# Tokenizer and scan stage of a four-stage kernel in one block, on one SBUF map drawn by hand

## The chip, the cores and the metric

The kernel runs on one core of one Trainium2 chip. The metric is the device time of one launch in microseconds (us), the median of three runs. The engines are TensorE (PE in the profile, its weight loads PEld), VectorE (DVE), ScalarE (ACT), GpSimd (POOL) and SyncE (SP), which here only issues DMAs and waits. Each engine runs its own instruction list in order; they meet at semaphores.

## The reference, cut to what matters

```python
# x [32,3,112,112], txt [32,32,192]
h = tokenizer(x)              # convs, wavelet packet, three depthwise+pointwise layers, layernorm; cls row first
h = concatenate([h, txt], 1)  # [32, 82, 192]: 1 cls + 49 patches + 32 text rows for each image
h = h + scan_layer(layernorm(h))   # selective scan (16 states, 384 channels), then a gated FFN
h = h + moe_layer(layernorm(h))    # 12-head attention, top-2 of 8 experts
# scan_layer(x): hn = rmsnorm(x) ; z = (hn @ W_in.T) * sigmoid(hn @ W_gate.T)
#   dt_in, Bm, Cm = split(z @ W_xproj.T) ; dt = softplus(dt_in @ W_dt.T + b_dt)
#   state[l] = exp(dt*A) * state[l-1] + (dt*z)*Bm ;  y = sum_s state*Cm + D*z ; ...
```

## The kernel before, in words

All values are float32. `H` [82 rows, 32 images, 192] stays in SBUF from the first stage to the last. There are four stages: `tokenizer`, `mamba` (the scan stage), `attention` with the routing, and `experts`. `mamba` and `attention` begin with a small block of their own, `row_stats`, for the mean and variance of each row of H. Each block ends at a barrier of all engines, and the SBUF and PSUM of one stage are given back before the next takes its own.

**Tokenizer.** Four chunks (`CH = 4`) of eight images (`IM = 8`) go through a software pipeline of seven waves (`w = 0..6`). In a wave DVE does the nine depthwise taps of several layers, one channel tile at a time (`dw`, L165 to L175: one TENSOR_SCALAR and eight SCALAR_TENSOR_TENSOR, accumulated in the PSUM bank psF). For the other tile ACT makes nine products (`weigh`, L337) in a ring of 14 and POOL adds them up (`add_up`, L478, eight dependent additions). PE does the pointwise layers (L232), and for the last layer 32 matmuls a chunk (L292), whose result comes out with the patches as rows. DVE takes these rows to `T0` (`take_rows`: L406 copies with a bias, L410 and L413 statistics), POOL makes the roots (`roots`, L465 and L467, POW), and DVE normalizes (`norm_rows`: eight L419, one L422, one L424). SP moves each finished chunk to H (L199).

In wave 5 DVE does: take_rows(1), the taps of the second fusion layer for chunk 3, the taps of the third for chunk 2, norm_rows(0). In wave 6: take_rows(2), the third layer's taps for chunk 3, norm_rows(1); then take_rows(3), norm_rows(2), norm_rows(3). When the chunks have landed, SP clears the semaphores and all engines meet (`retire`, L45).

**Scan stage.** `row_stats` (L529) takes 32 BN_STATS (L549) and 32 BN_AGGR (L552) on DVE and roots on POOL, while SP issues ten loads of weights and constants (L607). After a barrier DVE prepares constants, POOL makes the remaining roots (L1031 to L1040), and the 8 rounds of four images (`G = 4`, N = 328 columns) begin. A helper `program` writes the order: 16 steps (`STATE`), and in step s of round i each engine calls `step` (the scan of state s), `post` for the round before and `pre` for the round after. Round 0's `pre` has no scan beside it. Its parts by step number: 0 ACT makes `hn` (L861); 2 PE transposes it, ACT makes `hT`; 3, 4, 5 for each third of the channels two projections on PE (RG and RI, L756), a Tanh on ACT, a product `z` on DVE (L964); 6 two more products X1 and X0 (L764), `Bs` and `P3` on ACT, `R` on DVE (L969); 7 the low parts of P3; 8 and 9 step sizes on PE (L743), Relu, Abs and Exp on ACT; 10 Ln and two copies on ACT, then three additions on POOL (L1048, L1050, L1052) for `dt`; 11 one product on POOL for `dtz` (L1055). Then POOL makes `Bx` (L1075), ACT the decays (L935), and DVE runs the first scan (L1006). The projections of one pair of PSUM banks wait for the `z` before them.

`Bs` goes to memory and back as a broadcast `Bb` (L696, L700), and SP also zeroes an eighth of the expert buckets in each round (L705).

**Attention stage, its end.** For each of 8 rounds DVE's `place` writes the bucket slots of the tokens (L1553), and POOL scatters the rows with eight indirect DMAs (L1604). `slot` is one tile, so in the last round `place` waits for the scatters of the round before. POOL also adds the residual to H each round (L1620); SP writes H out (L1210).

Of the kernel before, what the change touches and what calls it, by code (L numbers as in the profile page):

```python
# [15 lines left out]
B = 32  # L16
# [28 lines left out]
def retire(nc, sems):  # L45

    for s in sems:
        nc.sync.sem_clear(s)
    nc.all_engine_barrier()
# [26 lines left out]
def tokenizer(nc, H, xcol, w_pl, w_pg, had, pw_mix, w96, vecs, pwb_row, lng_row, lnb_row, cls_row, txt):  # L76


    CH = 4
    IM = B // CH  # L80
    NP = IM * PATCHES
    ROW = GRID + 1
    IMG = ROW * ROW
    PADC = IM * IMG
    EDGE = ROW + 1
    ROWS = IM * ROW - 1
    with ExitStack() as ctx:
        def sb(name, shape, dt=F32):
            return ctx.enter_context(nc.sbuf_tensor(name, shape, dt))
# [12 lines left out]
        vec = sb("vec", [128, V_N])  # L102
# [6 lines left out]
        PRODUCTS = 14  # L109
# [14 lines left out]
        psC = ctx.enter_context(nc.psum_tensor("psC", [128, 3, BANK], F32))  # L124
        psA = ctx.enter_context(nc.psum_tensor("psA", [128, 2, BANK], F32))
        psB = ctx.enter_context(nc.psum_tensor("psB", [128, 2, BANK], F32))
        psF = ctx.enter_context(nc.psum_tensor("psF", [128, BANK], F32))
# [13 lines left out]
        s_mv = sem("a_mv"); s_rs = sem("a_rs"); s_t1 = sem("a_t1"); s_padp = sem("a_padp"); s_nh = sem("a_nh"); s_out = sem("a_out"); s_cls = sem("a_cls")  # L141
# [40 lines left out]
        ctx.callback(retire, nc, sems)  # L182
        block = ctx.enter_context(nc.Block())

        @block.sync
        def _(sp):
# [9 lines left out]
            sp.dma_start(H[1 + PATCHES:S, :, :], txt.rearrange("b t c -> t b c")).then_inc(s_cls, 16)  # L196
            for c in range(CH):
                sp.wait_ge(s_t1, c + 1)
                sp.dma_start(H[1:1 + PATCHES, c * IM:(c + 1) * IM, :], T0[:, c * IM:(c + 1) * IM, :]).then_inc(s_out, 16)  # L199
            sp.wait_ge(s_out, 16 * CH)  # L200
            sp.wait_ge(s_cls, 32)

        @block.tensor
        def _(pe):
# [32 lines left out]
            for w in range(WAVES):  # L237
                if w + 1 < CH:
                    conv(w + 1)
                if w < CH:  # L240
                    if w == 0:
                        pe.wait_ge(s_small, 16 * 3)
# [30 lines left out]
                if 0 <= w - 2 < CH:  # L273
# [6 lines left out]
                    pair(psA, wf[:, 2], lambda k: dense(DF[1], k)).then_inc(s_f[1], 1)  # L280
                if 0 <= w - 3 < CH:
# [14 lines left out]
        @block.scalar  # L296
        def _(act):
# [6 lines left out]
            act.wait_ge(s_small, 48)  # L304
# [35 lines left out]
            for w in range(WAVES):  # L340
                if w + 1 < CH:
                    gelu(w + 1)
                if 0 <= w - 1 < CH:
# [47 lines left out]
        @block.vector  # L391
        def _(v):
# [6 lines left out]
            v.wait_ge(s_small, 48)  # L399
            v.wait_ge(s_rows, 48)  # L400

            def take_rows(c):

                for n in range(c * IM // 2, (c + 1) * IM // 2):
                    v.wait_ge(s_f[2], n + 1)
                    v.tensor_tensor(T0[:, 2 * n:2 * n + 2, :], f3_bank[n % 3].rearrange("p (j c) -> p j c", j=2),  # L406
                                    rows[:, 0:1, :].broadcast_to([PATCHES, 2, D]), ALU.add).then_inc(s_t0, 1)
                v.wait_ge(s_t0, (c + 1) * IM // 2)
# [18 lines left out]
            for w in range(WAVES):  # L427
# [5 lines left out]
                if 0 <= w - 1 < CH:  # L433
# [3 lines left out]
                    dw(v, own, PF[0], DF[0], (0,), w - 1, V_F_DW, s_dwf[0])  # L437
                if 0 <= w - 4:
                    take_rows(w - 4)
                if 0 <= w - 2 < CH:  # L440
# [3 lines left out]
                    dw(v, own, PF[1], DF[1], (0,), w - 2, V_F_DW + 18, s_dwf[1])  # L444
                if 0 <= w - 3 < CH:
# [64 lines left out]
G = 4  # L510
# [1444 lines left out]
```

## Time and profile before

| | us |
|---|---|
| median of 3 runs (lowest, highest) | 1613.34 (1612.24, 1614.69) |
| the profiled execution: its time | 1608.27 |
| its span (first to last instruction) | 1606.4 |
| last tap of the tokenizer ends | 241.07 |
| tokenizer's last DVE instruction ends | 264.8 |
| first statistics of the scan stage begin | 272.4 |
| first scan of round 0 begins | 334.46 |
| last scatter of the attention stage is issued | 1305.8 |
| first instruction of the experts' stage on DVE | 1311.5 |

| engine | busy us | share of the span |
|---|---|---|
| PE | 1265.3 | 79% |
| DVE | 1033.7 | 64% |
| POOL | 764.3 | 48% |
| ACT | 708.1 | 44% |

Times of single instructions below are from this one profiled execution, whose time is 5.1 us under the median of the runs. Busy shares are averages over four stages with different limits; the places that matter here are the seam at 240 to 335 us and the end of attention at 1270 to 1312 us.

### The profile page before, as it was taken

How to read it: one execution, taken by the hardware profiler on the slowest of the kernel's cores; microseconds unless marked ns; L12 is line 12 of the kernel's file. 1: busy time of each engine (PE TensorE's matmuls, PEld its weight loads, DVE VectorE, ACT ScalarE, POOL GpSimd, SP SyncE). 2: the span in 40 equal slices, each digit the busy share in tenths (PEclk: the TensorE clock that was granted, in tenths of full speed). 3: DMA queues.
4: the chain of work that ended last, by engine and by line, in shares of the span. 5: the costliest groups of instructions: out<-in, count | busy, mean ns of one | idle time of the engine just before them, and what ended most of it. 6: DMA issues, size and time to landing. Idle time of an engine off the chain costs nothing. (4 is left out here: it accounts for less than half of the span.)

```text
span 1606.4 us, 19648 instructions
## 1 busy us (share of the span) xinstructions
PE 1265.3 (79%) x5818; PEld 834.7 (52%) x5819; DVE 1033.7 (64%) x1939; ACT 708.1 (44%) x1486; POOL 764.3 (48%) x500
## 2 busy tenths in 40 slices
PE   6786732456988989898878579888987529999996
PEld 4332321232554545455445348777876517777775
DVE  4699587168978889898898327776567512333332
ACT  1156620357758586776853135444442102222221
POOL 2038970387676676857672321144444632222222
PEclk9796775679989999999999779999797559999999
DMA  5100002123303030330300111121201112222221
GB/s 153 50 1 0 1 8 77 63 77 126 108 19 127 1 126 13 114 111 15 126 0 1 32 36 54 40 66 53 62 23 24 32 51 32 37 37 36 36 36 23
DMA packets 71571, 81.17 MB, mean 51 GB/s; under 512 B 13534, under 2 KB 63349, under 8 KB 71401
## 3 DMA queue, kind: packets, MB, share of 16 engines
q1 hardware_dynamic: 52210, 68.69, 13.7%
q0 software_dynamic: 17152, 9.24, 4.2%
q10 hardware_dynamic: 2136, 2.37, 0.5%
q8 instruction: 32, 0.52, 0.1%
q14 instruction: 41, 0.34, 0.1%
HBM read 48.93 MB, written 30.01 MB: 49 GB/s over the span
## 5 line engine op out<-in xcount | busy, mean ns | idle before, releaser
L1006 DVE TENSOR_TENSOR_SCAN hs<-b_ps,Bx 128x492 f32<-128x492 f32 x256 | 287.6, 1164 | 49.1 <-ACT b_ps L935 25.4
L1075 POOL TENSOR_TENSOR Bx<-dtz,Bb 128x984 f32<-128x984 f32 x128 | 289.3, 2279 | 56.8 <-DVE hs L1006 56.7
L935 ACT ACTIVATE b_ps<-dt,A 128x324 f32<-128x324 f32 (+1 forms) x512 | 214.1, 454 | 111.3 <-DVE hs L1006 106.0
L825 PE MATMUL b_ps<-hs,b_id 128*128 128x492 f32 x512 | 242.4, 597 | 9.2 <-DVE y L974 9.1
L1827 POOL DMA_INDIRECT out<-yt,dest x48 | 74.0, 1542 | 220.3 <-DVE yt L1814 215.0
L1015 DVE TENSOR_TENSOR hs<-hs,b_ps 128x984 f32<-128x984 f32 x128 | 150.2, 1174 | 2.6
L1708 PE MATMUL e_ps<-W,xT 97*128 (+1 forms) x384 | 138.5, 503 | 1.5 <-ACT xT L1762 1.0
L825 PEld LDWEIGHTS b_ps<-hs,b_id 128*128 128x128 f32 x512 | 94.2, 197 | 83.9 <-issue 81.6
L1800 DVE COPY hT_<-e_ps 128x768 f32<-128x768 f32 x48 | 45.9, 957 | 130.3 <-PE e_ps L1717 129.9
L1613 POOL TENSOR_TENSOR c_x<-c_x,bro 82x192 f32<-82x192 f32 x32 | 19.7, 615 | 195.2 <-DVE c_x L1456 194.7
L1727 PE MATMUL e_ps<-W,hT_ 128*128 x576 | 109.2, 327 | 0.9 <-DVE yb L1808 0.8
L795 PE MATMUL b_ps<-hfT,wug 96*128 96x328 f32 x256 | 85.2, 479 | 24.7 <-DVE av L991 24.0
L1604 POOL DMA_INDIRECT buckets<-XS,c_slot x64 | 90.4, 1412 | 27.1 <-issue 18.8
L1768 ACT ACTIVATE hb<-e_ps 128x768 f32<-128x768 f32 x48 | 38.9, 810 | 144.2 <-PE e_ps L1708 144.2
L1708 PEld LDWEIGHTS e_ps<-W,xT 97*128 97x128 f32 (+1 forms) x384 | 70.0, 192 | 55.0 <-issue 17.1
L1727 PEld LDWEIGHTS e_ps<-W,hT_ 128*128 128x128 f32 x576 | 91.4, 190 | 1.4 <-issue 1.4
L478 POOL TENSOR_TENSOR DF<-DF,prod 96x441 f32<-96x441 f32 x84 | 86.9, 1035 | 6.6
L813 PE MATMUL b_ps<-P,sel 96*128 96x328 bf16 x128 | 39.8, 312 | 59.2 <-DVE hs L1015 58.6
L795 PEld LDWEIGHTS b_ps<-hfT,wug 96*128 96x128 f32 x256 | 50.0, 203 | 64.5 <-DVE av L991 40.6
L1310 PEld LDWEIGHTS c_ps<-V,PT 82*82 82x82 f32 x768 | 69.2, 169 | 13.8 <-issue 7.6
L1762 ACT ACTIVATE xT<-e_ps,m_vec 96x128 f32<-96x128 f32 x96 | 38.4, 447 | 84.7 <-PE e_ps L1698 84.6
L1297 PE MATMUL c_ps<-kB,qT 128*82 128x328 f32 (+1 forms) x256 | 69.5, 422 | 2.0 <-DVE E L1427 2.0
(246 smaller groups left out, 2414.6 us busy)
## 6 DMA issues: line engine op xcount, KB each, us to landing
Bb<-b_rows SPq DMA_DIRECT2D x32, 656.0 KB, 7.1
buckets<-b_zero SPq DMA_DIRECT2D x8, 2288.0 KB, 15.6
xg<-buckets SPq DMA_DIRECT2D x48, 104.0 KB, 2.0
xc<-in_xcol SPq DMA_DIRECT2D x4, 1176.0 KB, 9.6
W<-in_w1d SPq DMA_DIRECT2D x8, 582.0 KB
W<-in_w2d SPq DMA_DIRECT2D x8, 576.0 KB
out<-H SPq DMA_DIRECT2D x8, 246.0 KB
H<-P SPq DMA_DIRECT2D x4, 294.0 KB
```

Of the source, the lines that this page charges most:

```text
L478: g.tensor_tensor(out, a, prod[:, (9 * n + t) % PRODUCTS], ALU.add).then_inc(s_sum, 1)
L795: mm = pe.matmul(ps[:, bank(name), 0:N], wug[:, k, w_, m * 128:(m + 1) * 128], hfT[:, k, :], start=k == 0, stop=k == 1)
L825: mm = pe.matmul(ps[:, BANK_Y + h, 0:HALF], ident[:], f2(hs[:, s % LONG])[:, h * HALF:(h + 1) * HALF], start=s == 0, stop=s == STATE - 1)
L935: a = act.activation(ps[:, BANK_A + h, c:c + w].rearrange("p (g t) -> p g t", t=S)[:, :, 1:S], dt[:, (par + t // STATE) % 2, m, g0 * S:g1 ...
L1006: v.tensor_tensor_scan(f2(hs[:, t % LONG])[:, c], ps[:, BANK_A + h, 0:HALF], f2(Bx[:, t % RING])[:, c], 0.0, ALU.mult, ALU.add).then_inc(s ...
L1015: v.tensor_tensor(hs[:, s % LONG], hs[:, s % LONG], ps[:, BANK_C + s % 2, 0:N].rearrange("p (a n) -> p a n", a=1).broadcast_to([128, NI, N ...
L1075: g.tensor_tensor(Bx[:, t % RING], dtz[:, p], Bb[:, p, t % STATE, :].rearrange("p (a n) -> p a n", a=1).broadcast_to([128, NI, N]), ALU.mu ...
L1297: mm = pe.matmul(ps[0:S, SCORES + h0 // 6, (h0 % 6) * S:(h0 % 6 + h1 - h0) * S], qT[:, par, m_, q * S:(q + 1) * S], kB[:, par, m_, q, j:j ...
L1604: g.indirect_dma_start(out=xs, out_offset=bass.IndirectOffsetOnAxis(ap=slot[:, k, c:c + 1], axis=0), in_=XS[:, par, c, :], in_offset=None) ...
L1708: mm = pe.matmul(ps[:, 1 + 2 * p + h, 0:384], xT[c_, p, k, :], W1[c_, k, bass.ds(e, 1), h * 384:(h + 1) * 384].rearrange("p a n -> p (a n) ...
L1727: mm = pe.matmul(ps[:, 7, 0:D], hT[:, p, k, :], W2[:, k, bass.ds(e, 1), :].rearrange("p a n -> p (a n)"), start=k == 0, stop=k == KF - 1)
L1827: g.indirect_dma_start(out=out, out_offset=bass.IndirectOffsetOnAxis(ap=dest[:, p:p + 1], axis=0), in_=yt[:, p, :], in_offset=None, comput ...
```

## The change

- Tokenizer and scan stage run in one block. The `retire` barrier and `row_stats` of the scan stage are gone (attention keeps its own). A function `places` gives every tile of both stages a fixed offset in one SBUF map; `vec` and `ident` are loaded once, at the start, so `ident` is one more DMA on SP's queue ahead of the image chunks. The ring of products shrinks from 14 to 13.
- The statistics are taken a chunk of eight images at a time, from H: `chunk_stats` on DVE, `chunk_roots` on POOL (one POW over both roots, 82x16, and one product).
- Hooks named `tail(point)` put round 0's first work into the tokenizer's instruction lists. DVE in wave 5: between the taps of chunk 3 and chunk 2, `chunk_stats(0)`, the halving of wzg and the cast of sel. DVE in wave 6: z of the first third inside take_rows(2), z of the second third ahead of the last taps; the third z and the memset ahead of norm_rows(3). POOL after wave 5: `chunk_roots(0)`. ACT ahead of its last nine products: `hn`. PE ahead of the last 32 matmuls: `pre` of steps 2, 3, 4. After the tokenizer DVE does R, the limit on A, `chunk_stats` 1 to 3, and then round 0's additions and product for dt and dtz, which were POOL's.
- `norm_rows(w - 5)` moves from the end of DVE's wave to its beginning.
- Loads: wzg, wx, wdt and oh are issued once the tokenizer's middle tiles are free (s_h at 4); A, wo and wdn after chunk 1 has gone to H; wug after chunk 3 has. SP clears the tokenizer's semaphores in round 0 once four engines have left it (`s_left`), ahead of the first zeroing of buckets.
- Attention: `slot` gets two halves, and the wait of the last `place` is gone; the last round's residual addition moves from POOL to DVE, after DVE's program.

```diff
-    for s in sems:
-        nc.sync.sem_clear(s)
-    nc.all_engine_barrier()
...
-        PRODUCTS = 14
+PRODUCTS = 13
...
+            sp.dma_start(ident[:], eye).then_inc(s_small, 16)
...
+                if 0 <= w - 5:
+                    norm_rows(w - 5)
                 if 0 <= w - 4:
                     take_rows(w - 4)
+                if w == WAVES - 1:
+                    tail("last taps")
...
+                if w == WAVES - 2:
+                    tail("last but one taps")
                 if 0 <= w - 3 < CH:
...
-                if 0 <= w - 5:
-                    norm_rows(w - 5)
             take_rows(CH - 1)
             norm_rows(CH - 2)
+            tail("last rows")
             norm_rows(CH - 1)
...
+            def chunk_stats(c):
+                a = slice(c * IM, (c + 1) * IM)
+                v.wait_ge(tok.s_out[c], 16)
+                for b in range(c * IM, (c + 1) * IM):
+                    n = own.did(v.bn_stats(st[:, b % IM, :], H[:, b, :]))
+                own.need(n)
+                for b in range(c * IM, (c + 1) * IM):
+                    n = own.did(v.bn_aggr(mv[:, b, :], st[:, b % IM, :]))
+                own.need(n)
+                own.did(v.tensor_scalar(r12[:, a], mv[:, a, 1], 1.0 + 1e-6, 1e-5 * 1e-6, ALU.mult, ALU.add))
+                own.did(v.tensor_scalar(r1[:, a], mv[:, a, 1], 1e-5, None, ALU.add))
+                own.did(v.tensor_scalar(negm[:, a], mv[:, a, 0], -1.0, None, ALU.mult))
+                own.need(own.n)
+                v.sem_inc(s_var, 1)
...
+            tok.vector(v, tail)
+            v.sem_inc(s_H, 2)
+            pre(0, 0, 6, None)
+            v.wait_ge(s_wA, 16)
+            v.tensor_scalar(f2(A[:]), f2(A[:]), 80.0, None, ALU.min).then_inc(s_A2, 1)
+            for c in range(1, CH):
+                chunk_stats(c)
+            program(v, first, step, pre, post, lambda last: drain(last, 1), done=(3, 4, 5, 6))
...
+            def chunk_roots(c):
+                a = slice(c * IM, (c + 1) * IM)
+                g.wait_ge(s_var, c + 1)
+                g.tensor_tensor(root[:, :, a], root[:, :, a], nh[:], ALU.pow).then_inc(s_root, 1)
+                g.wait_ge(s_root, c + 1)
+                g.tensor_tensor(nb[:, :, a], root[:, :, a], negm[:, a].rearrange("p (a b) -> p a b", a=1).broadcast_to([S, 2, IM]),
+                                ALU.mult).then_inc(s_r1, 1)
...
-                if isinstance(p, int) and p == ROUNDS - 1:
-                    v.wait_ge(s_sc, p * (16 * 2 * G))
-                v.tensor_copy(slot[:], sf[:]).then_inc(s_slot, 1)
+                v.tensor_copy(slot[:, p % 2], sf[:]).then_inc(s_slot, 1)
```

## Rows read from the trace of the kernel before

**Rows 1.** Windows: busy us (instructions) of PE, PEld, DVE, ACT, POOL; TensorE's granted clock; DMA

```profile
260.00:300.00 40.00, 5.71 (x16) 3.58 (x16) 18.09 (x76) 5.13 (x10) 13.18 (x11) 0.50 0.29 82
300.00:334.00 34.00, 13.42 (x37) 7.00 (x36) 1.98 (x4) 15.64 (x27) 12.06 (x8) 0.70 0.45 149
...
390.00:446.00 56.00, 48.75 (x168) 27.31 (x168) 48.87 (x52) 39.99 (x94) 38.66 (x20) 0.97 0.28 91
```

**Rows 2.** Timeline of the seam, 241 to 335 us: start, duration, what, [idle before <- releaser]

```profile
263.07 1.75 DVE L424 TENSOR_TENSOR P<-P,rows 49x1536 f32<-49x1536 f32 x1
...
272.43 8.41 DVE L549 BATCH_NORM_STATS2 b_st_stats<-H 82x6 f32<-82x192 f32 x32
...
280.87 2.21 DVE L552 BATCH_NORM_AGGREGATE b_mv<-b_st_stats 82x2 f32<-82x6 f32 x32
...
289.05 0.31 POOL L1031 TENSOR_SCALAR b_negm<-b_mv 82x32 f32<-82x32 f32 x1 [2.78 <-DVE wzg L956]
...
312.21 0.49 DVE L969 TENSOR_TENSOR R<-b_ps,P 64x328 f32<-64x328 f32 x1 [2.84 <-ACT P L876]
...
321.60 1.01 ACT L895 ACTIVATE ax<-ax 128x984 f32<-128x984 f32 x1
...
329.68 2.28 POOL L1055 TENSOR_TENSOR dtz<-dt,z 128x984 f32<-128x984 f32 x1
...
334.46 2.25 DVE L1006 TENSOR_TENSOR_SCAN hs<-b_ps,Bx 128x492 f32<-128x492 f32 x2 [21.77 <-POOL Bx L1075]
```

**Rows 3.** Timeline of POOL, waves 4 to 6 of the tokenizer

```profile
198.37 1.98 POOL L504 TENSOR_TENSOR PF<-L,R 96x392 f32<-96x392 f32 x2
200.31 0.96 POOL L478 TENSOR_TENSOR DF<-prod 96x441 f32<-96x441 f32 x1
201.34 7.64 POOL L478 TENSOR_TENSOR DF<-DF,prod 96x441 f32<-96x441 f32 x7
...
221.45 1.99 POOL L504 TENSOR_TENSOR PF<-L,R 96x392 f32<-96x392 f32 x2 [1.71 <-ACT R L387]
```

**Rows 4.** Timeline of DVE, waves 5 and 6 of the tokenizer

```profile
215.69 4.95 DVE L171 SCALAR_TENSOR_TENSOR psF<-PF,vec,psF 96x441 f32<-96x441 f32 x7
...
221.51 3.79 DVE L419 TENSOR_SCALAR P<-P,mv,rs 49x192 f32<-49x192 f32 x8 [0.16 <-DVE DF L171]
...
228.79 1.47 DVE L406 TENSOR_TENSOR P<-psC,rows 49x384 f32<-49x384 f32 x3
231.39 0.55 DVE L406 TENSOR_TENSOR P<-psC,rows 49x384 f32<-49x384 f32 x1 [1.12 <-PE psC L292]
231.97 2.17 DVE L410 BATCH_NORM_STATS2 st<-P 49x6 f32<-49x192 f32 x8
...
252.99 2.37 DVE L419 TENSOR_SCALAR P<-P,mv,rs 49x192 f32<-49x192 f32 x8
```

**Rows 5.** Timeline of PE: the last layer's matmuls, then round 0's projections

```profile
221.46 4.10 PE L292 MATMUL psC<-wf,DF 96*49 96x192 f32 x24 [1.19 <-DVEq L175]
...
241.18 8.42 PE L292 MATMUL psC<-wf,DF 96*49 96x192 f32 x32 [9.83 <-DVEq L175]
...
295.59 4.74 PE L756 MATMUL b_ps<-hT,wzg 96*128 96x328 f32 x8 [0.62 <-ACT hT L866]
...
306.29 2.47 PE L756 MATMUL b_ps<-hT,wzg 96*128 96x328 f32 x8 [0.66 <-DVE z L964]
```

**Rows 6.** Timeline of ACT in wave 3: the products of three tiles

```profile
137.85 15.04 ACT L337 ACTIVATE prod<-PF,vec 96x441 f32<-96x441 f32 x27
```

**Rows 7.** Timeline of POOL and DVE at the end of attention

```profile
1286.75 1.40 POOL L1604 DMA_INDIRECT buckets<-XS,c_slot  x1 [0.30 <-issue]
1292.45 1.40 POOL L1604 DMA_INDIRECT buckets<-XS,c_slot  x1 [4.29 <-DVE c_slot L1553]
...
1282.96 0.17 DVE L1548 TENSOR_REDUCE c_sf<-c_t 82x4 f32<-82x32 f32 x1
1291.97 0.17 DVE L1553 CAST c_slot<-c_sf 82x8 uint32<-82x8 f32 x1 [8.85 <-DMA buckets<-XS,c_slot]
```

More of the change, by code:

```diff
@@ L342, in _ @@
                     gelu(w + 1)
+                if w == WAVES - 1:
+                    tail("last wave")
                 if 0 <= w - 1 < CH:
@@ L659, in bank, with program @@
             return SIDE0 + PLACE[name] % SIDE
-        def program(engine, scan_first, step, pre, post, finish=lambda last: None, side_first=False):
+        def program(engine, scan_first, step, pre, post, finish=lambda last: None, side_first=False, done=(), late=lambda: None):
             def turn(i, par, s, last, has_post, has_pre):
@@ L673, in program @@
             for s in range(STATE):
-                pre(0, 0, s, None)
+                if s not in done:
+                    pre(0, 0, s, None)
             scan_first()
@@ L677, in program @@
                 turn(0, 0, s, False, False, True)
+            late()
             with engine.Fori(0, (ROUNDS - 2) // 2) as t:
@@ L690, in _, with tail @@
         def _(sp):
+            def tail(point):
+                if point == "stages over":
+                    for dst, src in ((wzg, w_zg), (wx, w_x), (wdt, w_dt), (oh, onehot)):
+                        sp.dma_start(dst[:], src).then_inc(s_w, 16)
+                if point == "last sums":
+                    sp.dma_start(A[:], a_log).then_inc(s_wA, 16)
+                    for dst, src in ((wo, w_o), (wdn, w_dn)):
+                        sp.dma_start(dst[:], src).then_inc(s_wo, 16)
+            tok.sync(sp, tail)
             for j in range(ROUNDS):
@@ L1021, in step, with tail @@
                     scan(i, s + 1)
-            program(v, first, step, pre, post, lambda last: drain(last, 1))
+            def tail(point):
+                if point == "last but one taps":
+                    v.wait_ge(tok.s_cls, 32)
+                    chunk_stats(0)
+                    v.wait_ge(s_w, 64)
+                    v.tensor_scalar(wzg[:, :, 0, :], wzg[:, :, 0, :], 0.5, None, ALU.mult).then_inc(s_cst, 1)
+                    v.tensor_copy(sel[:], oh[:, STATE:2 * STATE].rearrange("p (s a) -> p s a", a=1).broadcast_to([HD, STATE, 128])).then_inc(s_cst, 1)
+                if point == "last wave":
+                    v.wait_ge(tok.s_lr, CH)
+                    pre(0, 0, 3, None)
+                if point == "last taps":
+                    pre(0, 0, 4, None)
+                if point == "last rows":
+                    v.wait_ge(tok.s_t0, CH * IM // 2)
+                    v.memset(ps[:, BANK_A:BANK_A + 2, :], 0.0).then_inc(s_cst, 1)
+                    pre(0, 0, 5, None)
+            tok.vector(v, tail)
[6 more added lines that the diff above has]
+            program(v, first, step, pre, post, lambda last: drain(last, 1), done=(3, 4, 5, 6))
             v.wait_ge(s_H, 2 * ROUNDS + 2)
@@ L1085, in step, with tail @@
                     inputs(i, par, s + AHEAD)
+            def tail(point):
+                chunk_roots(0)
+            g.memset(nh[:], -0.5).then_inc(s_nh, 1)
+            g.wait_ge(s_nh, 1)
+            tok.gpsimd(g, tail)
+            for c in range(1, CH):
+                chunk_roots(c)
+            g.memset(zero[:], 0.0).then_inc(s_zero, 1)
             program(g, first, step, pre, post)
```

254 lines of the change are left out of this document (160 added, 94 removed).

## The prediction

> **What bounds the kernel now.** I read the stages as windows first, then the timeline of the seam, engine by engine, and then the end of attention.
>
> The windows [rows 1] show a pipeline that is nearly full in the scan rounds (DVE 48.9 and PE 48.8 of 56 us) and nearly empty at the seam: from 260 to 334 us DVE works 20.1 of 74 us, PE 19.1. The seam is a chain of single steps. The reader should see it in the timeline [rows 2]. The tokenizer's last normalization ends at 264.8. After that come the landing of its rows, the clearing of semaphores and a barrier, 7.6 us until 272.4. Statistics take until 283.1. POOL resumes at 289.05, held by constants and a second barrier: 6.0 us more. Then round 0's front runs from `hn` to `dtz` with nothing beside it, and the first scan starts at 334.46, after a wait of 21.77 us for POOL's Bx.
>
> From there on the rounds follow each other and every later stage starts from the one before it. So what the first scan gains is gained at the end, unless a round gives it back. The experts' stage is bound by PE and isn't touched.
>
> **What the change moves.** I walk DVE's new instruction list, because every other engine's new work is released by it or releases it. The start is 198.4, where POOL has the roots of chunk 0 (its next instruction starts at 198.37 [rows 3]); DVE is done with wave 4's taps by then. Clock times in this part are on the old time axis.
>
> 1. norm_rows(0), now first in wave 5. Alone its eight TENSOR_SCALARs take 2.37 us; beside two POOL additions they took 3.79 [rows 4], 1.4 more for two additions of 0.99, so about one of them got through per POOL instruction. At the new place POOL has those two additions and then sixteen more of about 1.03 us each, back to back [rows 3]. So: two of the eight at 1.0, six at 1.05, and the two long TENSOR_TENSORs at 1.75 each behind a POOL instruction of 1.0. 2.0 + 6.3 + 5.5 = 13.8 us. The lower bound is 5.9 (2.37 + 2 x 1.75: no collision); I take 13.8, since the measured row is the same instruction against the same kind of POOL instruction. POOL is held too, by at most 3.5 us, but has slack until the next rows need it.
>
> The Trainium skill has a rule for this (SBUF — State Buffer, section "Who interferes with whom"): a VectorE instruction in a two-port mode, or with two SBUF inputs beside a GpSimd instruction that reads SBUF, blocks and is blocked for whole instructions. By that rule, the row of 3.79 us agrees, norm_rows at its old place was nearly free of it and at its new place is not: it is the rule that speaks against this edit. Without it the sum would be the one with 5.9.
>
> 2. take_rows(1): 6.0 us, as from 228.79 to 234.8 (copies, a wait for a bank, statistics) [rows 4]. It now comes after norm_rows(0) instead of ahead of it, but its matmuls have long filled three banks.
> 3. Taps, chunk 3 of the second layer: 6.5 (7 x 0.71 and two ends of 0.7 [rows 4]).
> 4. chunk_stats(0): 8 x 0.263 and 8 x 0.069 from the rows of 32 [rows 2], three tiny instructions and four waits, 3.4. With the halving (0.54 before) and the cast (1.24): 5.4. H's chunk left at the end of step 1 and had 17 us to land (before it took 3.8). The weights were asked for at 168.
> 5. Taps, chunk 2 of the third layer: 6.4.
> 6. norm_rows(1), POOL idle: 6.1.
> 7. Copies of chunk 2 with the wait for the fourth bank: 3.1.
> 8. z of the first third. PE can transpose only after its last L292 of chunk 2, which the third copy freed. Transposes 0.8, hT 1.1, four products at full clock 2.5 (4.7 at half [rows 5]), z 0.5, latencies: 5.3 after the fourth copy. hn is ready by 237 (ACT waits for chunk_roots(0) behind POOL's last addition of L and R), so it isn't what is late.
> 9. Statistics of chunk 2, then z of the second third, whose products run meanwhile: 2.8 + 0.6.
> 10. Last taps: 6.5. They end near 261 instead of 241.07: this is where the inserted work goes, 20 us.
> 11. PE's 32 matmuls at half clock after its pause, 8.4, last copy 0.6: 9.0 [rows 5]. DVE waits through it; before, it did norm_rows(1) there.
> 12. Statistics 2.8, norm_rows(2) 5.9, memset and third z 1.5, norm_rows(3) 5.9: 16.1.
> 13. R and the limit on A: 0.9. PE has made X1 and X0 beside norm_rows(3).
> 14. chunk_stats 1 to 3: 3 x 3.4 = 10.2. The chain R, P3, step sizes, Exp, Ln on ACT takes 9.9 from R (312.7 to 322.6 before [rows 2]), so it is hidden under these by a hair; POOL's roots of each chunk (about 3.2: 0.156 a column from its POWs of 8 and 24 columns) trail by one and end before Bx.
> 15. Three additions and the product on DVE, 128x984 with two SBUF inputs: at the 1.14 us per 1000 columns of L424 [rows 2], 1.2 with its wait, 5.0 together. POOL took 9.3 for them (322.68 to 331.96).
> 16. First Bx 2.4.
>
> Sum: 13.8 + 6.0 + 6.5 + 5.4 + 6.4 + 6.1 + 3.1 + 5.3 + 3.4 + 6.5 + 9.0 + 16.1 + 0.9 + 10.2 + 5.0 + 2.4 = 106.1, so the first scan would start at 304.5.
>
> Two costs come earlier. The extra DMA ahead of the images: 0.5 (one issue on SP is 0.46, and PE did wait 1.8 for the images). The ring of 13: in wave 3 ACT's 27 products run without a stall [rows 6], the last at 152.3; POOL's sum that frees its place in a ring of 14 was done at 152.0, in one of 13 it is done at 153.1. 0.8 us, and ACT's later results then reach POOL's next additions with 0.2 to spare. I take both, 1.3; below it is nothing. First scan at 305.8: 28.7 us earlier.
>
> SP: b_rows goes out when its queue is past the last chunk, about 287; its broadcast lands 7 to 9 us later, before Bx at 302. wug, the clearing and the zeroing come after; the clearing of some 45 semaphores took 2.7 before. Round 1 needs its own B rows 20 us later. Hidden; if it weren't, DVE's second round would wait.
>
> **Attention.** POOL's last eight scatters start 4.29 us after the previous eight, behind the slot written at 1291.97, which waits for scatters to land [rows 7]; the values were there at 1283.1. With two halves the gap is 0.30: 4.0 us gained. The table for the experts follows the slot and moves ahead with it. The residual addition on DVE is under 2 us in a stretch where it idles 8.85.
>
> Total 32.7 us: 1575.6 for the profiled execution's 1608.27, and 1580.6 against the median, 5.1 above it.
>
> **Rivals.**
>
> A. No collision, and TensorE stays at its full clock. Step 1 costs 5.9, the 32 matmuls 5.5 (0.171 each as in the 24 of [rows 5]), the early costs are nothing: 7.9 + 2.9 + 1.3 more, 1568.5. For it: the clock was full for 24 matmuls there. Against it: the 3.79 us row, and PE pauses of 7 us ahead of both groups.
>
> B. The last waves hide nothing. The inserted pieces wait for each other (DVE for z, PE for hn, ACT for roots), and only the empty stretches vanish: 7.6 and 6.0 at the two barriers, 4.0 in attention: 1595.7. For it: steps 8 to 11 are a ring through four engines, and each of DVE's waits there delays taps that PE waits for. Against it: in my walk the products are the only wait of length, and the front between 289 and 334 is mostly steps that DVE didn't fill.
>
> C. Slower: the scan rounds start with TensorE at the lower of its two clock levels, 1.2 GHz, and it stays there. At 0.97 PE works 48.8 of 56 us [rows 1]; at 1.2 GHz that is some 95, so a round would last 40 us longer. It decides from 0.8 of a round at the low level on, which takes the 32.7 back; a whole round would give 1620. Against it: the granted clock before was 0.50 in the idle seam and still 0.89 in the first 56 us of rounds.
>
> D. The change doesn't do what it says: DVE, now with the statistics, the sums and the z's, is the only thing that matters, and new waits add up to the 32.7. No such wait is in the rows; 1612 to 1615.
>
> **How the numbers follow.** Forecast 0.60, A 0.14, B 0.20, C 0.04, D 0.02. The forecast's own range is 1574 to 1588: down by half of the collision and part of the clock, up by 2.2 for each of the two pairs of products at half clock and 3 for waits between small instructions. A reaches to 1568 and B to 1596; I leave out B's last two us and what is below 1568: 1568 to 1594. Faster by over 0.2% (3.2 us, about what a measurement of this kernel can tell from no change) 0.94, within it 0.02, slower 0.04.
>
> **What the next profile would show.** The L419 group of chunk 0 near 199 us at 8 us or more for eight (right) or near 2.4 (A). Last taps ending near 262 (if near 245, step 8 was dear for nothing; if past 268, B). The 32 last matmuls at about 8.4. DVE without a wait over 1 us between its last normalization and dt. First scan at 306. The eight-scatter groups 0.3 apart, and DVE's first instruction of the experts 32.7 earlier than 1311.45. I am wrong if the scan starts early and the rounds (56 us each) grow, or if chunk_stats waits for H to land.

## The result

| kernel | median us (lowest to highest) | ratio to the kernel before, 95% interval |
|---|---|---|
| before, beside it | 1612.79 (1610.33 to 1614.69), 4 runs | |
| changed | 1570.53 (1567.64 to 1572.95), 4 runs | 0.9743 [0.9728, 0.9758] |
| changed, on another occasion | 1571.0 (1567.61 to 1573.25), 5 runs | 0.9756 [0.9734, 0.9777] |

The change makes the kernel 40 to 42 us faster (on the second occasion the kernel before had 1610.74). Ratios leave out two executions in a slow state, one of the kernel before (1841.87 us) and one of the attention edits alone (2253.55 us), at mean granted clocks of 0.69 and 0.55 where the others have 0.87 to 0.89. The two profiled executions are 35.3 us apart (1608.27 and 1572.95). Cut at points that both have, they give:

| part (us) | before | changed | gained |
|---|---|---|---|
| start to the first scan | 334.46 | 305.37 | 29.09 |
| first scan to attention's first statistics (the rounds) | 578.94 | 576.09 | 2.85 |
| attention stage, to the experts' first DVE instruction | 398.05 | 394.79 | 3.26 |
| experts' stage | 294.95 | 294.85 | 0.10 |

The seam in windows of the changed kernel (us, busy us and count of PE, PEld, DVE, ACT, POOL, granted clock, DMA), where DVE had worked 18.1 of 40 us and 2.0 of 34 [rows 1]:

```profile
260.00:300.00 40.00, 16.95 (x58) 9.91 (x58) 32.37 (x108) 14.37 (x23) 11.13 (x7) 0.71 0.24 79
300.00:334.00 34.00, 25.81 (x80) 13.61 (x81) 30.48 (x30) 20.09 (x49) 27.60 (x15) 0.79 0.32 99
```

DVE's timeline of the changed kernel, the answers to [rows 2, 4]:

```profile
201.12 9.52 DVE L429 TENSOR_SCALAR P<-P,mv,rs 49x192 f32<-49x192 f32 x8 [4.24 <-POOL rs L481]
210.67 2.65 DVE L432 TENSOR_TENSOR P<-P,rows 49x1536 f32<-49x1536 f32 x1
213.35 1.75 DVE L434 TENSOR_TENSOR P<-P,rows 49x1536 f32<-49x1536 f32 x1
...
218.46 0.55 DVE L414 TENSOR_TENSOR P<-ps,rows 49x384 f32<-49x384 f32 x1 [1.96 <-PE ps L300]
...
228.37 2.17 DVE L1014 BATCH_NORM_STATS2 b_st<-H 82x6 f32<-82x192 f32 x8 [0.23 <-DVE DF L176]
...
239.85 2.40 DVE L429 TENSOR_SCALAR P<-P,mv,rs 49x192 f32<-49x192 f32 x8 [0.16 <-DVE DF L176]
...
252.43 0.50 DVE L1030 SCALAR_TENSOR_TENSOR z<-sg,ps 128x328 f32<-128x328 f32 x1 [3.52 <-PE ps L784]
...
261.67 0.67 DVE L176 SCALAR_TENSOR_TENSOR DF<-PF,vec,ps 96x441 f32<-96x441 f32 x1
265.29 0.55 DVE L414 TENSOR_TENSOR P<-ps,rows 49x384 f32<-49x384 f32 x1 [2.95 <-PE ps L300]
...
286.54 0.48 DVE L1035 TENSOR_TENSOR R<-ps,P 64x328 f32<-64x328 f32 x1
...
297.55 1.18 DVE L1038 TENSOR_TENSOR ax<-u,ax 128x984 f32<-128x984 f32 x1 [0.56 <-ACT ax L933]
...
301.20 1.18 DVE L1045 TENSOR_TENSOR dtz<-dt,z 128x984 f32<-128x984 f32 x1
305.37 2.25 DVE L1082 TENSOR_TENSOR_SCAN hs<-ps,Bx 128x492 f32<-128x492 f32 x2 [2.98 <-POOL Bx L1173]
```

The reader is to see three things. The eight L429 of chunk 0 take 9.52 us, those of chunk 1 at a place where POOL is idle 2.40. Between the last tap and the first scan DVE has no wait over 3 us. The wait in front of the first scan is 2.98 us for one Bx instead of 21.77. POOL beside the first rows, PE around the last matmuls (answers to [rows 3, 5]), and ACT:

```profile
204.06 7.64 POOL L492 TENSOR_TENSOR DF<-DF,prod 96x441 f32<-96x441 f32 x7
218.50 1.11 POOL L492 TENSOR_TENSOR DF<-prod 96x441 f32<-96x441 f32 x1 [6.80 <-PE ps L300]
```

```profile
239.81 8.52 PE L300 MATMUL ps<-wf,DF 96*49 96x192 f32 x32 [6.58 <-DVEq L180]
...
249.83 2.44 PE L784 MATMUL ps<-hT,wzg 96*128 96x328 f32 x8 [0.81 <-ACT hT L904]
...
262.45 7.46 PE L300 MATMUL ps<-wf,DF 96*49 96x192 f32 x32 [7.00 <-DVEq L180]
```

```profile
290.90 1.28 ACT L927 ACT_TABLE_LOAD   x1
292.20 1.02 ACT L927 ACTIVATE u<-ax 128x984 f32<-128x984 f32 x1
```

The end of attention, POOL, then DVE (answers to [rows 7]): the wait of 4.29 us between the groups of eight is gone, and one issue takes 2.12 us beside DVE's residual addition.

```profile
1251.39 2.12 POOL L1713 DMA_INDIRECT buckets<-XS,c_slot  x1 [0.30 <-issue]
...
1255.52 1.40 POOL L1713 DMA_INDIRECT buckets<-XS,c_slot  x1 [0.30 <-issue]
1257.22 1.40 POOL L1713 DMA_INDIRECT buckets<-XS,c_slot  x1 [0.30 <-issue]
```

```profile
1251.29 0.95 DVE L1702 TENSOR_TENSOR H<-H,XN 82x768 f32<-82x768 f32 x1
```

### The profile page after: what moved, and what is told of

It reads as the page before. It is cut to its first block and busy times, and to the rows that moved or that the text cites. A ratio compares the mean times of both kernels' runs of the same rounds, so it can differ in the third digit from the quotient of the medians.

```text
span 1571.1 us, 19634 instructions
## 1 busy us (share of the span) xinstructions
PE 1263.1 (80%) x5818; PEld 832.9 (53%) x5819; DVE 1044.7 (66%) x1955; ACT 708.8 (45%) x1486; POOL 755.3 (48%) x493
## 5 line engine op out<-in xcount | busy, mean ns | idle before, releaser
L1082 DVE TENSOR_TENSOR_SCAN hs<-ps,Bx 128x492 f32<-128x492 f32 x256 | 287.6, 1164 | 30.4 <-ACT ps L973 25.4
L973 ACT ACTIVATE ps<-dt,A 128x324 f32<-128x324 f32 (+1 forms) x512 | 214.1, 454 | 106.5 <-DVE hs L1082 104.9
L856 PE MATMUL ps<-hs,b_id 128*128 128x492 f32 x512 | 243.3, 598 | 9.2 <-DVE y L1050 9.1
L1092 DVE TENSOR_TENSOR hs<-hs,ps 128x984 f32<-128x984 f32 x128 | 150.2, 1174 | 2.6
L856 PEld LDWEIGHTS ps<-hs,b_id 128*128 128x128 f32 x512 | 94.4, 198 | 84.5 <-issue 82.3
L823 PE MATMUL ps<-hfT,wug 96*128 96x328 f32 x256 | 83.7, 472 | 24.8 <-DVE av L1067 24.1
L841 PE MATMUL ps<-P,sel 96*128 96x328 bf16 x128 | 40.2, 316 | 54.8 <-DVE hs L1092 41.0
L823 PEld LDWEIGHTS ps<-hfT,wug 96*128 96x128 f32 x256 | 49.1, 199 | 64.0 <-DVE av L1067 40.7
L1419 PEld LDWEIGHTS c_ps<-V,PT 82*82 82x82 f32 x768 | 69.3, 169 | 13.8 <-issue 7.6
L1532 DVE TENSOR_REDUCE mx<-c_ps 82x12 f32<-82x984 f32 x32 | 37.7, 1177 | 51.7 <-PE c_ps L1406 51.4
```

Source lines behind the costliest of these rows:

```text
L823: mm = pe.matmul(ps[:, bank(name), 0:N], wug[:, k, w_, m * 128:(m + 1) * 128], hfT[:, k, :], start=k == 0, stop=k == 1)
L856: mm = pe.matmul(ps[:, BANK_Y + h, 0:HALF], ident[:], f2(hs[:, s % LONG])[:, h * HALF:(h + 1) * HALF], start=s == 0, stop=s == STATE - 1)
L973: a = act.activation(ps[:, BANK_A + h, c:c + w].rearrange("p (g t) -> p g t", t=S)[:, :, 1:S], dt[:, (par + t // STATE) % 2, m, g0 * S:g1 ...
L1082: v.tensor_tensor_scan(f2(hs[:, t % LONG])[:, c], ps[:, BANK_A + h, 0:HALF], f2(Bx[:, t % RING])[:, c], 0.0, ALU.mult, ALU.add).then_inc(s ...
L1092: v.tensor_tensor(hs[:, s % LONG], hs[:, s % LONG], ps[:, BANK_C + s % 2, 0:N].rearrange("p (a n) -> p a n", a=1).broadcast_to([128, NI, N ...
L1419: mm = pe.matmul(ps[0:S, HEAD_OUT + c % 2, h * (DH + 1):(h + 1) * (DH + 1)], PT[:, c % 2, h, :], V[:, vpar, c, h, :], start=True, stop=True)
```

## The experiments

The line numbers in their profiles are their own. All are edits of the changed kernel, but for the first. "First scan" and "rounds" are cut as in the table above. Each was timed beside the kernel before, which the ratios compare it with; the changed kernel stood beside some of them only, and the median of the kernel before moved between 1609.34 and 1612.79 us from one occasion to another. "First tap" is the tokenizer's first depthwise instruction on DVE; counting from it leaves out what an execution draws in its first 30 us.

**The attention edits alone, and all but them.** The first is the kernel before with the two halves of `slot` and the moved addition; the second is the changed kernel with these undone.

```diff
-                if isinstance(p, int) and p == ROUNDS - 1:
-                    v.wait_ge(s_sc, p * (16 * 2 * G))
-                v.tensor_copy(slot[:], sf[:]).then_inc(s_slot, 1)
+                v.tensor_copy(slot[:, p % 2], sf[:]).then_inc(s_slot, 1)
```

> The kernel before with the two attention edits alone: slot in two halves, the last residual addition on DVE. By my sum the last scatters start 4.0 us earlier; by the trace of the changed kernel 3.3, since one scatter issue took 2.12 instead of 1.40 us beside the addition. So 3 to 4 us faster. The rival, that the scatters in flight only queue up in the DMA engines, gives under 1 us.

> The changed kernel without the attention edits. By the trace they are worth 3.3 us: last scatter near 1272.5 in a run whose scan rounds take 576 us, 3 to 4 us slower than the changed kernel. If the gain beyond the profile's 35.3 us were theirs, 7 us or more.

Alone: 1608.01 us, ratio 0.9978 [0.9963, 0.9993], attention stage 395.07 us. Undone: 1573.02 (1571.76 to 1575.11), ratio 0.9771 [0.9755, 0.9787], attention stage 398.08, and the wait is back in POOL's timeline:

```profile
1251.49 1.40 POOL L1713 DMA_INDIRECT buckets<-XS,c_slot  x1 [0.30 <-issue]
1257.16 1.40 POOL L1713 DMA_INDIRECT buckets<-XS,c_slot  x1 [4.28 <-DVE c_slot L1662]
```

Profiles with and without the edits are 3.0 to 3.3 us apart in this stage. The times say it less sharply: 2.7 us between the medians and 3.5 by the ratio (1.1 to 6.0) for the edits alone, 2.0 to 2.5 for the kernel without them, where 3 to 4 was expected. Under 1 us, the rival, is not what happened.

**The changed kernel again.** The same program, to see what an execution draws for itself.

> The changed kernel again, against the kernel before, to size the gain over many executions. The two profiled executions differ by 35.3 us (first scan 29.1 earlier, scan rounds 2.9, attention's end 3.3), the medians so far by 42.3. If the trace holds the whole gain, the timed difference is 34 to 38 us. If something that a single profile doesn't show adds to it (fewer stretches at a lower granted clock, for one), it stays near 42.

1571.0 us. Its first scan came at 302.52, its rounds took 576.24, the attention stage 394.77. The first scan moved by 2.85 us with nothing changed. This execution still ended within 0.7 us of the other (1572.30 and 1572.95), because its experts' stage took 296.97 us for 294.85. The timed gain of 39.7 us lies between the two that were named (34 to 38, and 42).

**ident last.** The DMA of `ident` goes behind the image chunks again.

```diff
-            sp.dma_start(ident[:], eye).then_inc(s_small, 16)
...
             sp.dma_start(H[1 + PATCHES:S, :, :], txt.rearrange("b t c -> t b c")).then_inc(s_cls, 16)
+            sp.dma_start(ident[:], eye).then_inc(s_cls, 16)
```

> The changed kernel with the load of ident issued behind the images instead of ahead of them. The first convolution started 0.45 us later than before and took 13.78 instead of 12.09 us. If the extra DMA caused both, through the pause ahead of the convolution and the clock granted after it, the wave starts and the first scan come 2.1 us earlier (303.2). If the slow convolution was a matter of the single execution, 0.5 us earlier (304.9).

1570.64 us (1568.13 to 1577.42), ratio 0.9753 [0.9733, 0.9774]: no different. The first scan came at 304.05, between the 303.2 and 304.9 that were named. The profiled execution was the longest of the five (1577.42), with rounds of 581.82 us, 5.7 more than the changed kernel's: one profile doesn't tell what a kernel's rounds take. The first tap of the tokenizer came at 31.07 us; in the changed kernel at 32.81 and 31.34, in the kernel before at 30.67, and at 33.03 in the kernel with the attention edits alone, whose start is the kernel before's. So the early 2 us belong to an execution, and what ident costs is below that. Counted from the first tap, the first scan comes at 303.8 us before (302.5 with the attention edits alone) and 272.6 and 271.2 changed: the seam itself gives about 31 us.

**The norm where POOL is less busy.** norm_rows(0) goes between the taps of chunks 3 and 2, `chunk_stats(0)` behind them.

```diff
-                if 0 <= w - 5:
-                    norm_rows(w - 5)
+                if w == WAVES - 1:
+                    norm_rows(1)
...
-                    tail("last but one taps")
+                    norm_rows(0)
                 if 0 <= w - 3 < CH:
...
+                if w == WAVES - 2:
+                    tail("last but one taps")
```

> The changed kernel with norm_rows(0) behind the taps of chunk 3 instead of at the beginning of wave 5, and chunk_stats(0) with the constants behind the taps of chunk 2. If the collision with POOL's additions is the cost, norm_rows(0) takes 6 to 8.5 us instead of 13.9, the taps of chunk 2 end near 232 instead of 239.7; some of it goes again, since the 5 us of statistics and constants then stand with norm_rows(1) under PE's 32 matmuls: first scan 2 to 4 us earlier. If norm_rows is slow for its place in the order alone, it takes 13.9 again and the first scan is no earlier.

1578.33 us (1574.53 to 1580.17), ratio 0.9801 [0.9779, 0.9822]: 7 us slower than the changed kernel, though the collision was nearly halved. DVE, then PE, of this kernel:

```profile
215.99 4.72 DVE L429 TENSOR_SCALAR P<-P,mv,rs 49x192 f32<-49x192 f32 x8 [0.16 <-DVE DF L176]
220.75 1.75 DVE L432 TENSOR_TENSOR P<-P,rows 49x1536 f32<-49x1536 f32 x1
222.53 2.53 DVE L434 TENSOR_TENSOR P<-P,rows 49x1536 f32<-49x1536 f32 x1
...
252.30 0.50 DVE L1032 SCALAR_TENSOR_TENSOR z<-sg,ps 128x328 f32<-128x328 f32 x1 [5.83 <-PE ps L786]
```

```profile
231.46 7.92 PE L300 MATMUL ps<-wf,DF 96*49 96x192 f32 x24 [10.19 <-DVEq L180]
243.09 2.80 PE L300 MATMUL ps<-wf,DF 96*49 96x192 f32 x8 [3.71 <-DVE P L414]
...
247.81 4.34 PE L786 MATMUL ps<-hT,wzg 96*128 96x328 f32 x8 [0.67 <-ACT hT L906]
```

The step is 9.0 us instead of 13.9, and the taps of chunk 2 end 8.3 us earlier (231.4 for 239.7; 1.9 of it is an earlier first tap). But chunk 2's matmuls then start with the norm still ahead of the copies that free their banks (3.71), and the first pair of products runs at half clock (4.34 for 2.44). z comes at 252.30, in the changed kernel at 252.43. Everything won on DVE was waited away before the last taps. The last 32 matmuls then took 8.53 us for 7.46, and the first scan came at 306.33, 1.0 later where 2 to 4 earlier was expected; the step itself was expected at 6 to 8.5. The rounds, 580.59 us, took the rest.

**Nothing of round 0 in the waves.** All hooks run after the tokenizer's last normalization; one block, the order of the norms, the sums on DVE and attention stay.

```diff
-            tok.vector(v, tail)
+            tok.vector(v, lambda point: None)
+            for point in ("last but one taps", "last wave", "last taps", "last rows"):
+                tail(point)
```

> The changed kernel with every hook's work placed behind the tokenizer's last instruction on its engine (statistics of chunk 0, constants, hn, transposes, projections, the first z's); the common block, the order of norm_rows, the sums on DVE and the attention edits stay. If the last waves hide that work, the tokenizer's last normalization ends near 275.5 instead of 286.5 and the front from statistics to dtz is in the open again: first scan near 322 instead of 305.4 and about 16 us slower than the changed kernel (ratio to the kernel before 0.985). If only the barriers mattered (rival B), the first scan stays within 3 us of 305.4.

1590.33 us (1587.26 to 1597.48), ratio 0.9884 [0.9864, 0.9904]; first scan at 322.20. DVE:

```profile
281.76 1.21 DVE L1108 CAST sel<-oh 96x2048 bf16<-96x2048 f32 x1
293.00 0.49 DVE L1032 SCALAR_TENSOR_TENSOR z<-sg,ps 128x328 f32<-128x328 f32 x1 [10.03 <-PE ps L784]
```

The hooks are worth 16.8 us of the first scan (322.20 to 305.37; 18.4 when counted from the first tap) and 19 to 20 of the time (15.8 between the two profiled executions). The chain hn, transpose, products, which the waves hid, stands open here as one wait of 10.03 us and further ones of 2.6, 1.5 and 2.8.

**The sums of round 0 on POOL.**

```diff
-                if s == 10 and isinstance(j, int) and j == 0:
...
-                    v.tensor_tensor(f2(dt[:, par]), f2(rl[:]), f2(ax[:]), ALU.add).then_inc(s_dt, 1)
-                    v.wait_ge(s_dt, 1)
-                    v.tensor_tensor(f2(dtz[:, par]), f2(dt[:, par]), z[:, par, :], ALU.mult).then_inc(s_dtz, 1)
```

> The changed kernel with round 0's three additions and the product for dt and dtz on POOL again. They were 4.9 us on DVE and 9.3 us on POOL in the kernel before, and POOL is behind the roots of chunk 3 and P3 until 303. If they stand on the path, first scan 6 to 8 us later (312). If ACT's chain or the roots set the time anyway, under 3 us.

1589.82 us (1587.58 to 1592.04), ratio 0.9873 [0.9854, 0.9893]. The first scan:

```profile
311.71 2.25 DVE L1072 TENSOR_TENSOR_SCAN hs<-ps,Bx 128x492 f32<-128x492 f32 x2 [16.08 <-POOL Bx L1163]
```

It is 6.3 us later than in the changed kernel, but the time is about 19 us longer, and the rounds took 587.25 us for 576.09. The windows of all eight rounds, of the changed kernel and then of this one:

```profile
305.37:881.46 576.09, 494.16 (x1756) 283.56 (x1756) 493.45 (x541) 371.37 (x870) 377.20 (x187) 0.97 0.21 66
311.71:898.96 587.25, 504.40 (x1756) 289.28 (x1756) 494.22 (x541) 370.80 (x870) 377.06 (x187) 0.95 0.20 64
```

PE is busy 10.2 us longer for the same 1756 matmuls; DVE, ACT and POOL are within 0.8 us. The extra time stands in whole stretches in which the same instructions run under a lower granted clock. Two stretches of four steps in this kernel, then the same two in the changed one:

```profile
656.12:674.25 18.13, 14.79 (x57) 9.18 (x57) 15.98 (x19) 9.68 (x24) 9.45 (x5) 0.91 0.01 1
707.85:729.48 21.63, 18.52 (x64) 11.86 (x63) 16.88 (x20) 10.02 (x25) 20.16 (x9) 0.84 0.00 0
```

```profile
645.30:661.27 15.97, 13.12 (x57) 8.26 (x57) 15.78 (x19) 9.68 (x24) 9.45 (x5) 1.00 0.00 0
694.88:713.65 18.77, 15.66 (x64) 10.07 (x63) 16.69 (x20) 10.22 (x25) 18.62 (x9) 1.00 0.00 0
```

2.2 and 2.9 us more, and PE's busy time grew by 1.7 and 2.9. What causes it is asked in the next two experiments.

**The rounds later, nothing else moved.** DVE writes dtz two or five times more, ahead of all eight rounds.

```diff
+                    for again in range(5):
+                        v.tensor_tensor(f2(dtz[:, par]), f2(dt[:, par]), z[:, par, :], ALU.mult).then_inc(s_pad, 1)
+                        v.wait_ge(s_pad, again + 1)
```

> The same with two more instructions: the rounds start later by 2.4 us (first scan about 305.0 to 307.8), about where the kernel with the norm between the taps had it (306.33; its rounds took 580.59). Theory 1 (the clock that the rounds get depends on when they start): rounds of 578 us or more, and a time of 1576 to 1580, more than the 2.4 us inserted. Theory 2 (the start costs itself and nothing more): rounds of 576 us, time 1573.5.

> The changed kernel with VectorE writing dt times z five more times in front of the first scan (the same values, each waiting for the one before): nothing else of the seam moves, only the four rounds start later by 5 x 1.2 = 6.1 us, so the first scan comes at about 308.6 to 311.5, where the kernel with the sums on GpSimd had it (311.71). That kernel's rounds took 587.25 us against 576.09, all of it in stretches of the same instructions under a lower granted clock. Theory 1 (which stretches get the full clock depends on when the rounds start): the rounds take 580 us or more here too, and the time is near 1582 to 1590. Theory 2 (GpSimd's sums themselves cost the rounds those 11 us, by what they leave queued on GpSimd and SyncE): the rounds take 576 us, and the time is 1571 + 6 = 1577.

| inserted us | first scan | rounds | median | over the changed kernel's 1570.5 to 1571.0 |
|---|---|---|---|---|
| 2.4 | 307.85 | 580.33 | 1578.23 (1576.03 to 1580.2) | 7.2 to 7.7 |
| 6.1 | 311.28 | 577.45 | 1582.47 (1580.57 to 1585.17) | 11.5 to 12.0 |

Ratios 0.9791 [0.9774, 0.9807] and 0.9827 [0.9809, 0.9845]. By the medians both cost about 5 us more than was inserted, by the ratios 3 to 5 and 5 to 7: a delay of the rounds isn't worth itself alone. Theory 1 holds for both medians. It misses the profile of the longer delay, whose rounds of 577.45 are short of the 580 that it named; and since that kernel starts its rounds where the one with POOL's sums does, the start doesn't explain 11 us. The medians say the same: 1589.82 with POOL's sums, 1582.47 here.

**The kernel with POOL's sums again.**

> The kernel with round 0's sums on GpSimd once more, unchanged, on another occasion. Its rounds took 587.25 us in its profile, 11 more than the changed kernel's, in stretches of the same instructions at a lower granted clock, and its median was 18 us above the changed kernel's though its first scan is only 6.3 later. Delaying the changed kernel's rounds by 6 us gave rounds of 577.45 and 10 to 12 us in the medians. Theory 1 (the clock grants belong to one execution: each profile draws its own): first scan at 310 to 312, rounds anywhere in 575 to 587 and most likely near 578 to 582, but a median near 1583 as for the delayed kernel. Theory 2 (something in this kernel costs its rounds 11 us every time): rounds of 585 or more again, in the same stretches, and a median of 1588 to 1591.

1590.32 us (1587.3 to 1591.93), ratio 0.9857 [0.9837, 0.9878]; first scan at 312.29, rounds 586.02. Theory 2 holds in its size: it is this kernel and not this execution. Its stretches weren't all the same (20.09 us at 0.92 in place of the 21.63 at 0.84). Beyond round 0 the two programs have the same instructions. Why one finds more low stretches, 350 us after the place where they differ, no run shows.

**A front drawn earlier still.** The third z and R stand ahead of chunk 2's norm, and three of the four chunk_stats before the sums; chunk_stats(3) stands behind dtz. The rows of B are issued earlier on SP.

```diff
+                if point == "waiting for rows":
+                    chunk_stats(1)
+                if point == "third z":
+                    pre(0, 0, 5, None)
                 if point == "last rows":
                     v.wait_ge(tok.s_t0, CH * IM // 2)
+                    pre(0, 0, 6, None)
...
                     v.tensor_tensor(f2(dtz[:, par]), f2(dt[:, par]), z[:, par, :], ALU.mult).then_inc(s_dtz, 1)
+                    chunk_stats(3)
```

> An attempt at a faster version: the third z ahead of norm_rows(2), R ahead of norm_rows(3), the cast of sel and the statistics of chunk 1 where DVE waits for PE, the statistics and roots of chunk 3 behind dtz, and B's rows sent ahead of the last chunk. In the changed kernel ACT's chain (10.9 us from R to the last copy) ended 0.6 us after DVE's last statistics, so both must move. If these two set the first scan, R comes 6 us earlier and the first scan is at 298 to 300. If B's rows or POOL set it, 303 to 305.

1573.02 us (1571.42 to 1576.98), ratio 0.9775 [0.9757, 0.9792]. R came 8 us earlier (278.5), but the first scan came at 302.17, in neither of the ranges named: two new delays stood in front of it, a wait for chunk 3's rows, issued late, and a tiny instruction held beside POOL's first Bx. The rounds took 579.08 us.

```profile
295.73 2.17 DVE L1025 BATCH_NORM_STATS2 b_st<-H 82x6 f32<-82x192 f32 x8 [1.37 <-DMA H<-P]
...
298.61 3.09 DVE L1030 TENSOR_SCALAR b_root<-b_mv 82x8 f32<-82x8 f32 x1
...
302.17 2.25 DVE L1094 TENSOR_TENSOR_SCAN hs<-ps,Bx 128x492 f32<-128x492 f32 x2 [0.34 <-DVE b_negm L1032]
```

**The same with chunk 3's statistics behind the first scan.**

```diff
             def first():
                 v.sem_inc(s_left, 1)
                 scan(0, 0)
+                chunk_stats(3)
```

> As the kernel with the front drawn earlier (third z, R and the statistics of chunk 1 ahead of chunk 2's norm; three chunks' statistics ahead of the first scan), but chunk 3's statistics stand behind the first scan, not in front of it: there they waited 1.37 us for rows that SyncE had sent late, and their 3.09 us tiny instruction lay beside GpSimd's first products. Bx was ready by about 297.3, so the first scan should come at 297.5 to 298.5 (302.17 in that kernel), and the second follows 3.3 us later than usual. If only the work in front of the first scan counts, the rounds as a whole gain 1.4 + 2.6 = 4.0 us on that kernel, and the time is about 1569 to 1570, 1.5 to 3 us under the changed kernel. Rival: the granted clock of the rounds changes with their start, and takes back or adds steps of 1.3 to 1.7 us, so the time lands between 1566 and 1576 and the first scan tells nothing of it.

1573.63 us (1570.21 to 1574.66), ratio 0.9761 [0.9746, 0.9777]. Both delays are gone and the first scan is where it was expected:

```profile
297.44 2.25 DVE L1093 TENSOR_TENSOR_SCAN hs<-ps,Bx 128x492 f32<-128x492 f32 x2 [2.51 <-POOL Bx L1187]
```

Its rounds took 583.47 us, of which the moved statistics are 3.4. Counted from the first tap the first scan is 8.4 us earlier than in the changed kernel and attention's start 1.0; of the 5.0 that should have remained (8.4 less 3.4), 4.0 are gone. PE is busy for 498.46 us in these rounds, in the changed kernel's for 494.16, with the same 1756 matmuls. Another 1.9 us of both fronts' profiled times is the experts' stage, 296.7 to 296.8 us as in the changed kernel's second profile. So neither front beats the changed kernel: what they win in front of the first scan comes back in the rounds. The rival named ahead of the run is what happened.

## Why the prediction was right, point by point

The mechanism and most terms held. The number did less well: 1570.5 us lies below the forecast's own range of 1574 to 1588, and inside the stated 1568 to 1594 only because that was drawn out to reach rival A. Its sixteen steps against DVE's timeline of the changed kernel, each from its first instruction to the next step's:

| step | predicted | measured |
|---|---|---|
| 1 norm_rows(0) beside POOL | 13.8 | 13.9 |
| 2 take_rows(1) | 6.0 | 6.8 |
| 3 taps | 6.5 | 6.6 |
| 4 chunk_stats(0), halving, cast | 5.4 | 5.0 |
| 5, 6 taps, norm_rows(1) | 12.5 | 12.4 |
| 7, 8 copies, z of the first third | 8.4 | 7.1 |
| 9, 10 statistics, second z, last taps | 9.9 | 9.5 |
| 11 the 32 matmuls | 9.0 | 8.2 |
| 12, 13 two norms, third z, R, A | 17.0 | 16.5 |
| 14 chunk_stats 1 to 3 | 10.2 | 10.5 with its wait |
| 15 sums | 5.0 | 4.8 |
| 16 Bx | 2.4 | 3.0 |
| sum | 106.1 | 104.3 |
| start of step 1 | 198.4 + 1.3 | 201.1 |
| first scan | 305.8 | 305.37 |

That the first scan is off by 0.4 us only is in part luck: the steps took 1.8 us less than their sum, and the first of them began 1.4 us later. The changed kernel's other profile has the first scan at 302.52.

- **The collision.** Priced at 13.8 against 5.9 without it, measured 13.9. Its parts missed by 1.1 to 1.2 each and cancelled: the eight TENSOR_SCALARs took 9.52 where the sum had 8.3, the two long instructions 4.40 where it had 5.5, because POOL's additions stopped at 211.7 and the second met none. The rule that spoke against the edit (the Trainium skill, SBUF — State Buffer, "Who interferes with whom") agrees with the 9.52 us here and with the 4.72 where fewer additions stood beside it. What the sum didn't ask was whether moving it away would pay. It didn't: the step lay ahead of waits for PE that took its place.
- **Step 2.** The wait for the fourth bank was 1.96, not 1.12. POOL's next eight additions waited for the matmuls that needed the same bank (6.80), so ten POOL instructions stood beside the norm, not eighteen. The others fell beside the taps of step 3, which took 0.71 us each all the same.
- **The clock at the two places where I had bounds.** The products of step 8 ran at full clock (2.44), the 32 matmuls at a mix (7.46 between 5.5 and 8.4).
- **The chain on ACT.** It was said to be hidden under chunk_stats "by a hair". It ended 0.56 us after them: a table load of 1.28 us in front of Exp is in no term of mine, and without it the chain would have ended 0.7 us ahead of them (an estimate from these two numbers).
- **POOL ahead of Bx.** The roots were to end before Bx. POOL was through with them and with P3 at 303.01, 0.6 us after dtz, and that is the 3.0 for 2.4 of step 16. Two of its instructions took longer there, beside DVE's sums: 1.15 us for 0.22 and 1.62 for the 0.80 of before.
- **The early costs.** 1.3 us predicted; step 1 began 2.7 late. 2.1 of these were there at the first tap, and they go with the execution. The ring of 13 explains at most 0.6.
- **The seam as a whole.** 28.7 predicted, 29.1 in the profiled pair, about 31 when the start's luck is taken out. Rival B (the waves hide nothing) is refuted by the kernel that runs the hooks afterwards: it is 16.8 us later at the first scan, 18.4 from the first tap. Rival A fails at its first term, the collision, though its time of 1568.5 is nearer to the median than mine: right total, wrong reason. D is refuted with it.
- **Attention.** 4.0 predicted, 3.26 in the profile. The wait went as said; 0.7 came back in one scatter issue of 2.12 us beside the residual addition, which I had placed in an idle stretch of DVE and not looked at from POOL's side. All twelve profiles with the edit have this one issue at 2.12 or 2.13, the two without it have none over 1.66.
- **The rounds.** Taken as unchanged, with C as the only way in which they could move. They moved the other way by 2.85 us in this pair. A round isn't 56 us either, which was the length of the window in [rows 1]: the changed kernel's began at 645.3, 713.7 and 782.0, 68.35 us apart where the granted clock was 1.00, and rounds with a low stretch took up to 73.4 (with POOL's sums). C's price for a round is too low by that, and nothing else rests on it. Over thirteen profiles of kernels whose rounds have the same instructions they lie between 574.8 and 587.3, in steps of some 1.3 to 2.9 us, each a stretch at a lower granted clock.
- **The median.** Of the 10.1 us between 1580.6 and 1570.5, 2.6 is the profiled pair (0.4 seam, 2.85 rounds, less 0.7 attention, 0.1 after). The other 7.5 is the offset: I carried over that the profiled execution of before lay 5.1 under its median, while that of the changed kernel lay 2.4 over its own. The mis-sized term is this offset, with the rounds: one execution's clock grants were treated as the kernel's property. Other medians of the kernel before are 1609.3 to 1612.8.

What stays open: why a kernel's rounds draw more or fewer low stretches. The delays show that it isn't neutral to when the rounds begin, the repeated kernel that it is partly a property of the program. An effect of the pause in front of the rounds would fit the two fronts, but no run varied the pause alone.

## What to carry to other kernels

Walk the engine that carries the inserted work, instruction by instruction, with each wait: sixteen terms from rows of before gave the stretch from the first of them to the first scan to 1.8 of 106 us, and hiding a serial front in another stage's waves was worth 18 of the 31 us. An edit that shortens one engine's list ahead of a wait gains nothing until the engine waited for is earlier too: 6.4 us won on DVE became waits for PE. And where a stage is bound by matmuls under a clock that comes and goes, predict the difference with a band of several us that no instruction accounts for; compare medians with medians, not one profile's offset carried over.

## What the runs showed of the hardware

- **Short instructions suffer most in a collision.** Eight TENSOR_SCALARs of 49x192 took 9.52 us beside nine POOL additions of about 1 us, and 2.40 alone: nearly one for each POOL instruction. A TENSOR_SCALAR of 82x8 took 3.09 us beside two of POOL's Bx (2.2 us each), for 0.17 alone. It works both ways: an indirect DMA issue of 1.40 us on POOL became 2.12.
- **Clock grants come in steps.** A granted clock of 1.00 is 2.4 GHz; the values between are stretches spent partly at 1.2 GHz. The same instructions of four scan steps took 15.97, 17.67 or 18.13 us at granted clocks of 1.00, 0.90 and 0.91, and another stretch 18.77, 20.09 and 21.63 at 1.00, 0.92 and 0.84. DVE's and ACT's busy times there are the same to 0.2 us; PE is what stretches. The experts' stage, which no edit touched, shows such a step too: 294.9 to 295.3 us in ten profiles (PE busy 275.5 to 275.7) and 296.7 to 297.0 in four (277.1), its 1344 matmuls the same.
- **A table load moved.** Before, the load (1.28 us) stood at 286.0 in front of the Exp of A, where ACT had been idle, and round 0's Tanh and Exp needed none. The changed kernel's Tanh ran in the tokenizer's last wave without one of its own, A's Exp comes later, and so the load stands in front of the first Exp, at 290.90, in the chain.

One of the stretches of the changed kernel at a lower clock:

```profile
575.25:592.92 17.67, 14.81 (x57) 8.83 (x57) 15.91 (x20) 9.69 (x24) 8.08 (x5) 0.90 0.00 0
```

The Trainium skill (TensorE: Matmul & The Clock Gate, Part 1) says that the gate's observation runs freely, so that a change of level falls at a point that varies. By that rule executions of one program differ, as the two profiles of the changed kernel do. It doesn't say why one program should be slower than another: the medians of the delayed kernels, 5 us over what was inserted, and the eight timed executions with POOL's sums, all between 1587.3 and 1592.0, don't follow from it alone, and no run here shows the phase itself.
